# Two layers of graph message passing: which tensor the node update stores, where x2 and the residual base are formed, and how far ahead sources are prepared

## The reference, cut to what matters

```
h  = relu(layernorm(x));   x2 = x + rgcn(rgcn(h))     # each rgcn layer ends in a relu
h  = relu(layernorm(x2))
for each edge: msg = layernorm(relu(relu([h[src], h[dst], edge] @ eW1 + eb1) @ eW2 + eb2)) * eg + ebeta
agg = segment_sum(msg, dst)
upd = relu([h, agg] @ nW1 + nb1) @ nW2 + nb2
out = x2 + layernorm(h + upd) * ng + nbeta
```

## Time and profile before

| | us |
|---|---|
| median of 3 runs | 2960.8 (2960.65 to 2963.27) |
| profiled execution, its own time | 2965.21 |
| span of the profile | 2963.5 |
| node update, first load issued to the message pass's first gather | 1546.1 to 1841.2 |
| message pass, up to the last pass's first load | 1841.2 to 2549.3 |
| last node pass | 2549.3 to 2963.5 |

### The profile page before, as it was taken

One profiled execution on the slowest core, in us unless ns is written; L12 is line 12 of the kernel. 1 busy time (PEld: TensorE's weight loads), 2 busy tenths in 40 slices (PEclk: granted clock), 3 DMA queues, 4 the chain that ended last, 5 costly groups with the idle time before them and its releaser, 6 DMA issues. The chain is left out here.

```text
span 2963.5 us, 56389 instructions
## 1 busy us (share of the span) xinstructions
PE 2203.0 (74%) x16219; PEld 1880.8 (63%) x16219; DVE 2125.7 (72%) x7344; ACT 1585.1 (53%) x3382; POOL 2016.0 (68%) x1479
## 2 busy tenths in 40 slices
PE   4778988888578898888835665677777777566765
PEld 4678988888578898888835554444444444454553
DVE  6878877777333677666628775677777777499999
ACT  5996655555333444444417766444444443467774
POOL 6754777655667288888767773688877776455555
PEclk9999999999889999999978888899998988799998
DMA  7985555555389545555439998345444443466663
GB/s 245 313 287 132 108 103 101 99 86 95 39 319 365 177 86 86 87 87 86 77 66 400 412 409 324 84 85 94 84 91 84 84 91 50 144 192 191 197 197 131
DMA packets 268196, 473.22 MB, mean 160 GB/s; under 512 B 62736, under 2 KB 142288, under 8 KB 268112
## 3 DMA queue, kind: packets, MB, share of 16 engines
q1 hardware_dynamic: 158352, 382.24, 39.4%
q0 software_dynamic: 109760, 90.00, 20.0%
HBM read 291.28 MB, written 180.81 MB: 159 GB/s over the span
## 5 line engine op out<-in xcount | busy, mean ns | idle before, releaser
L1135 POOL DMA_INDIRECT s<-E_summed,c_scat x392 | 654.2, 1669 | 285.8 <-ACT E_summed L1314 164.9
L1363 PE MATMUL ps<-c_w,E_masked 128*128 128x128 f32 x6272 | 722.1, 276 | 3.2 <-DVE E_masked L1166 3.2
L1363 PEld LDWEIGHTS ps<-c_w,E_masked 128*128 128x128 f32 x6272 | 713.6, 193 | 4.0 <-DVE E_masked L1166 4.0
L1166 DVE SCALAR_TENSOR_TENSOR E_masked<-E_type_row,E_hT 128x512 f32<-128x512 int32 x784 | 484.6, 688 | 79.4 <-ACT E_hT L1283 66.9
L366 POOL DMA_INDIRECT E_src_rows<-s,c_src x392 | 414.9, 1058 | 166.5 <-issue 118.0
L1473 POOL DMA_INDIRECT s<-E_summed,c_scat x196 | 320.9, 1637 | 107.9 <-issue 56.4
L366 POOL DMA_INDIRECT E_src_rows<-in_x,c_src x196 | 192.9, 984 | 103.5 <-issue 74.2
L1462 POOL DMA_INDIRECT E_ends<-x,c_near x196 | 198.2, 1011 | 95.7 <-issue 57.3
L1314 ACT COPY E_summed<-ps 128x512 f32<-128x512 f32 x98 | 57.5, 586 | 374.9 <-DMA s<-E_summed,c_scat 374.9
L572 PE MATMUL ps<-c_sl,N_hT 128*128 128x128 f32 x1568 | 199.9, 282 | 18.1 <-DVE N_out L407 13.0
L1378 PE MATMUL ps<-E_msg,E_same 128*128 128x128 bf16 (+1 forms) x2450 | 207.3, 241 | 1.3 <-DVE E_msg L1216 1.3
(11 more groups left out here) (142 smaller groups left out, 4787.5 us busy)
## 6 DMA issues: line engine op xcount, KB each, us to landing
s<-N_out SPq DMA_DIRECT2D x147, 512.0 KB, 4.9
N_xin<-in_x SPq DMA_DIRECT2D x98, 512.0 KB, 13.1
N_sin<-s SPq DMA_DIRECT2D x98, 512.0 KB, 5.6
E_dst_row<-in_dst_line SPq DMA_DIRECT2D x147, 256.0 KB, 4.8
E_type_row<-in_type SPq DMA_DIRECT2D x98, 256.0 KB, 3.9
N_xin<-s SPq DMA_DIRECT2D x49, 512.0 KB, 6.1
x<-N_x SPq DMA_DIRECT2D x49, 512.0 KB, 11.3
N_xin<-x SPq DMA_DIRECT2D x49, 512.0 KB, 4.0
```

The source lines that it names most:

```text
L1135: pool.indirect_dma_start(s, bass.IndirectOffsetOnAxis(ap=c["scat"][:, k:k + 1], axis=0), summed[:, g % 2, t * D:(t + 1) * D], None, compu ...
L1166: nc.vector.scalar_tensor_tensor(out=masked[:, u % 2, r, :], in0=type_row[:, u, :], scalar=float(r), in1=hT[:, u % 2, :], op0=ALU.is_equal ...
L1363: ins = nc.tensor.matmul(ps[:, 2 + u % 2, t * D:(t + 1) * D], masked[:, u % 2, r, t * P:(t + 1) * P], w[:, r, :], start=(r == 0 and t == 0 ...
```

## The change

The node update forms x2 in place of s2, lets ScalarE normalise all eight rows with the relu in it, and stores h instead of x2. The copies of the product move from ScalarE to VectorE. Statistics are no longer kept. SP's order and the wait ahead of a load change.

The message pass gathers h for the destination ends, so only the four source tiles are normalised, and these now two groups ahead. SP also loads s2 and x again, group by group; VectorE forms x2 (`update`) and adds nbeta (`add_nbeta`), and SP stores the result as `base`. The turn of the next group comes ahead of the out layer on TensorE. The order on ScalarE and VectorE changes, and the buffer of sums is four deep. GpSimd's list of gathers and scatters is the same.

The last node pass loads h, s3 and base. GpSimd and the activations that formed h are gone. TensorE transposes into one pair of banks and has three pairs for the sums; ScalarE normalises all eight rows; VectorE multiplies by ng and adds the base, a group later. Base and result buffers are two deep. It is written out without a loop. Of the other stages only the zero fill of the tables' last rows changes: its source is 128 columns, read five times.

```diff
-                sp.dma_start(a[s][NODES:ROWS_S, :].rearrange("(p k) d -> p (k d)", k=DUMP_FOLD),
-                             zeros[:]).then_inc(loaded, 16)
+                sp.dma_start(a[s][NODES:ROWS_S, :].rearrange("(p k) d -> p k d", k=DUMP_FOLD),
+                             each_tile(zeros, DUMP_FOLD)).then_inc(loaded, 16)
             for out, in_ in loads:
...
             def load(i, u):
-                wait(sp, x2_ready, UNROLL * i + u - 3)
+                wait(sp, h_ready, UNROLL * i + u - 3)
                 sp.dma_start(sin[:, u, :], rows(a["s2"], node_base(i, u))).then_inc(loaded[u], 16)
                 sp.dma_start(xin[:, u, :], rows(a["x"], node_base(i, u))).then_inc(loaded[u], 16)
-            def store_x2(i, u):
+            def store_h(i, u):
                 g = UNROLL * i + u
                 if isinstance(g, int) and g == GROUPS_N - 1:
...
+                sp.dma_start(rows(a["h"], node_base(i, u)), h[:, u, :]).then_inc(h_stored[u], 16)
...
                         load(0, k)
-                m, n = ahead(i, u, -2), ahead(i, u, 4)
-                store_x2(i, u)
+                    store_h(0, 0)
+                m, l, n = ahead(i, u, -1), ahead(i, u, 1), ahead(i, u, 4)
                 if n:
                     load(*n)
+                if l:
+                    store_h(*l)
                 if m:
                     store(*m)
             sweep(sp, step)
-            for g in (GROUPS_N - 2, GROUPS_N - 1):
...
+            def scales(i, u):
+                ln.reciprocals(nc, dve, u, UNROLL * i + u)
+                ln.shifts(nc, u)
+            def results(i, u, half):
+                g = UNROLL * i + u
+                if half == 0:
+                    wait(dve, stored[u % 2], 16 * (2 * i + u // 2))
+                dve.wait_ge(product, 2 * g + half + 1)
+                nc.vector.tensor_copy(out[:, u % 2, half * 512:(half + 1) * 512],
+                                      ps[:, 4 + 2 * (u % 2) + half, :]).then_inc(out_ready, 1)
             def step(i, u):
                 if first(i, u):
-                    updated(0, 0)
-                    halves(0, 0)
...
+                        if k < 2:
+                            scales(0, k)
                 n, m = ahead(i, u, 3), ahead(i, u, 2)
                 if n:
-                    both(n, m)
-                elif m:
-                    reciprocals(*m)
-                    ln.shifts(nc, UNROLL * m[0] + m[1])
-                    normalise(*m, range(NT - ON_ACT)).then_inc(normed, 1)
+                    updated(*n)
+                if m:
+                    scales(*m)
+                if n:
+                    g = UNROLL * n[0] + n[1]
+                    halves(*n)
+                    ln.sums(nc, dve, g)
+                results(i, u, 0)
+                if n:
+                    ln.means(nc, dve, n[1], g)
+                results(i, u, 1)
+                if n:
+                    ln.totals(nc, dve, n[1], g)
             sweep(dve, step)
...
                 act.wait_ge(ln.shift_ready, g + 1)
-                wait(act, turned, 2 * (g - 1))
-                for k in range(NT - ON_ACT, NT):
+                wait(act, turned, 2 * (g - 3))
+                wait(act, h_stored[u], 16 * i)
+                for k in range(NT):
                     cols = slice(k * D, (k + 1) * D)
-                    ins = ln.scaled(nc, h[:, u % 2, cols], x2[:, u, cols], k, g, ACT.Identity)
-                ins.then_inc(act_normed, 1)
+                    ins = ln.scaled(nc, h[:, u, cols], sin[:, u, cols], k, u, ACT.Relu)
+                ins.then_inc(h_ready, 1)
...
+            def load(g):
+                u = g % UNROLL
+                wait(sp, product, 2 * (g - 3))
+                sp.dma_start(sin[:, u, :], rows(a["s3"], at(g))).then_inc(loaded[u], 16)
+                sp.dma_start(hin[:, u, :], rows(a["h"], at(g))).then_inc(loaded[u], 16)
+            def load_base(g):
+                u = g % 2
+                wait(sp, out_ready, 2 * (g - 1))
+                sp.dma_start(base[:, u, :], rows(a["base"], at(g))).then_inc(based[u], 16)
...
+            for g in range(GROUPS_N):
+                if g + 4 < GROUPS_N:
+                    load(g + 4)
+                if g >= 1:
+                    store(g - 1)
+                    if g + 1 < GROUPS_N:
+                        load_base(g + 1)
...
+            for g in range(GROUPS_N):
+                if g + 2 < GROUPS_N:
+                    hidden_rows(g + 2, 0)
+                ln.deviations(nc, act, c["eps"], g % UNROLL, g)
+                if g + 2 < GROUPS_N:
+                    hidden_rows(g + 2, 1)
+                outer_norm(g)
...
+            for g in range(GROUPS_N):
+                residual(g, 0)
+                if g + 1 < GROUPS_N:
+                    turn(g + 1)
+                residual(g, 1)
+                update(g, 0)
+                update(g, 1)
...
+            def scale(g, half):
                 cols = slice(half * 512, (half + 1) * 512)
-                nc.vector.tensor_tensor(res[:, u, cols], res[:, u, cols], base[:, u, cols],
+                dve.wait_ge(normed, 2 * g + half + 1)
+                if half == 0:
+                    wait(dve, out_ready, 2 * g)
+                nc.vector.tensor_tensor(tiles_of(scaled[:, cols]), tiles_of(normal[:, g % 2, cols]),
+                                        each_tile(c["ng"], NT // 2), ALU.mult).then_inc(scaled_ready, 1)
+            def finish(g, half):
+                u = g % 2
+                cols = slice(half * 512, (half + 1) * 512)
+                if half == 0:
+                    dve.wait_ge(based[u], 16 * (g // 2 + 1))
+                    wait(dve, stored[u], 16 * (g // 2))
+                dve.wait_ge(scaled_ready, 2 * g + half + 1)
+                nc.vector.tensor_tensor(res[:, u, cols], scaled[:, cols], base[:, u, cols],
                                         ALU.add).then_inc(out_ready, 1)
...
+            for g in range(GROUPS_N):
+                halves(g)
+                statistics(g)
+                if g:
+                    scale(g - 1, 0)
+                scales(g)
+                if g:
+                    scale(g - 1, 1)
+                    finish(g - 1, 0)
+                    finish(g - 1, 1)
...
+            def load_base(i, u):
+                wait(sp, base_stored[u % 2], 16 * (2 * i + u // 2))
+                sp.dma_start(base[:, u % 2, :], rows(a["s2"], node_base(i, u))).then_inc(base_loaded[u % 2], 16)
+                sp.dma_start(base_x[:, u % 2, :], rows(a["x"], node_base(i, u))).then_inc(base_loaded[u % 2], 16)
+            def store_base(i, u):
+                g = UNROLL * i + u
+                last_store(sp, base_stored, g)
+                sp.wait_ge(base_step, 2 * g + 2)
+                sp.dma_start(rows(a["base"], node_base(i, u)), base[:, u % 2, :]).then_inc(base_stored[u % 2], 16)
             def step(i, u):
                 if first(i, u):
                     for k in range(3):
                         load(0, k)
-                n = ahead(i, u, 3)
+                    load_base(0, 0)
+                m, n, l = ahead(i, u, 1), ahead(i, u, 3), ahead(i, u, -1)
                 if n:
                     load(*n)
+                if l:
+                    store_base(*l)
+                if m:
+                    load_base(*m)
             sweep(sp, step)
+            store_base(GROUPS_N // UNROLL, 0)
...
                     pool.indirect_dma_start(
-                        ends[:, u, GE + t * D:GE + (t + 1) * D], None, a["x2"],
+                        ends[:, u, GE + t * D:GE + (t + 1) * D], None, a["h"],
...
                         a["s3"], bass.IndirectOffsetOnAxis(ap=c["scat"][:, k:k + 1], axis=0),
-                        summed[:, g % 2, t * D:(t + 1) * D], None, compute_op=ALU.add).then_inc(added, 16)
+                        summed[:, g % UNROLL, t * D:(t + 1) * D], None, compute_op=ALU.add).then_inc(added, 16)
...
                 wait(dve, act_normed, UNROLL * i + u - 3)
-                lx.variances(nc, dve, [ends[:, u, t * D:(t + 1) * D] for t in range(2 * GT)], u, UNROLL * i + u)
-            def normalise(i, u):
+                lx.variances(nc, dve, [ends[:, u, t * D:(t + 1) * D] for t in range(GT)], u, UNROLL * i + u)
+            def scales(i, u):
                 lx.reciprocals(nc, dve, u, UNROLL * i + u)
                 lx.shifts(nc, u)
-                for t in range(GT, 2 * GT):
-                    tile = ends[:, u, t * D:(t + 1) * D]
-                    ins = lx.normalise(nc.vector, tile, tile, t, u)
-                ins.then_inc(normed, 1)
+            def update(i, u):
+                dve.wait_ge(base_loaded[u % 2], 32 * (2 * i + u // 2 + 1))
+                nc.vector.scalar_tensor_tensor(out=base[:, u % 2, :], in0=base[:, u % 2, :], scalar=0.0,
+                                               in1=base_x[:, u % 2, :], op0=ALU.max, op1=ALU.add).then_inc(base_step, 1)
+            def add_nbeta(i, u):
```

(31 more changed lines are left out.)

403 lines of the change are left out of this document (129 added, 274 removed).

## The result

The changed kernel takes 2857.0 us in the median of four runs (2854.4 to 2859.3), the one before 2960.7 beside it (2959.5 to 2963.3): ratio 0.9651, 95% interval 0.9639 to 0.9663. The prediction was 2850 us, range 2815 to 2905. The profiled execution of the changed kernel has a span of 2853.5 us against 2963.5, 110 us less. I cut both spans at the same marks, read from the time lines: GpSimd's first gather of the node update (0.7 us after the first load), the first gather of the message pass, the last pass's first load.

A forecast was written before the change was run, and what follows sets the result against it. Transfers were taken to bound the node update, GpSimd's issues (95% occupied) the message pass, with compute close, and VectorE, waiting for GpSimd, the last pass. Terms 0 + 2 + 2 - 115 = -111 us gave 2850 us, range 2815 to 2905.

The forecast's parts named there:

- Zero fill: At the very start: 512-byte pieces in place of 2.5 KB ones, costed at 0, bounds -1 to +1 us.
- Node update: Node update stage: transfers set the pace, so 0, plus 2 us for the tail; bounds -5 and +20 us.
- Message pass, compute side: Message pass: the compute engines need 13.0 to 13.8 us a group, taken as 13.3, against 13.6 now.
- The waits for sums: Message pass, GpSimd: its 21 us of waits for sums go, since compute at 13.3 us a group no longer limits it.
- the 2 us foreseen: Message pass: prologue 2 us earlier, with half the statistics ahead of the first turn.
- Message pass, GpSimd: Message pass: GpSimd's work goes from 661 to 665 us, +4, or +2 with the prologue; bounds -20 and +31.
- twice the work of that kind adds 0 to 18 us; I take 6: Message pass: more two-input VectorE operations lengthen GpSimd's scatter issues by 0 to 18 us, taken as 6.
- The waits for landing: Message pass: added transfers raise GpSimd's waits for scatters to land from 13.7 us to 30, between 14 and 47.
- Rival 3: Message pass loses 35 to 45 us by low clock and added VectorE work, or by scatter waits: 2890 us, chance 0.11.
- its own criterion: Prediction is wrong if the last pass takes over 320 us or the message pass moves by more than 30.
- Last pass: Last node pass: without GpSimd's work, 5.7 us a group (bounds 5.4 and 6.5), 299 us against 414, so -115.
- Rival 1: Last pass: transfers bind it at 6.4 us a group, so the stage takes 333 us and the total 2884; chance 0.16.

The follow-up runs named there:

- b_form: Kernel before, with the dump-row fill reading 128 columns of zeros five times and the tile kept at 640 columns, so no buffer moves: ratio 0.9972.
- a_none: Changed kernel without any base work in the message pass (no loads, VectorE operations or store); last pass loads h instead: 2780 us, stage 635.8 us.
- a_nodve: Changed kernel without VectorE's two operations on the base rows in the message pass, all transfers kept: 50 us faster by medians.
- a_gathers4: Changed kernel with all four gathers of a group issued ahead of all four scatters in the message pass: 2809 us, 48 us faster in the median.
- a_n3_noscale: Changed kernel without VectorE's product by ng in the last pass: tail 269.9 us, median 4.4 us below that of the changed kernel.
- b_nopool3: Kernel before, without GpSimd's two operations in the last pass: the tail falls from 421.5 to 298.3 us.
- a_pieces: Changed kernel with each of VectorE's two operations on the base rows cut into four pieces: runs of 2802.8, 2803.6, 2832.4 and 2838.1 us.

## Why the prediction was right, and where not

**Zero fill, 0 (bounds -1 to +1): wrong.** It is worth 8 us. The step looked only at what the fill delays at the start, and that is indeed nothing: the first edge pass begins its scatters at 258.7 us in the kernel before and in b_form.

**Node update, +2: -1.8, right.** The transfers are as full as before (DMA share 1.03 at 417 GB/s); the later loads cost nothing that shows.

**Message pass, compute side: right as far as it can be seen.** The waits for sums, 21 us, were to vanish: with the new order alone 6.2 are left (a_none). That a_none gains 24 is not this term alone, since 9 of it are waits for landing. What the compute side needs by itself was not measured, since GpSimd set the pace in every kernel. TensorE is idle ahead of the pair sums, as foreseen (103.6 us), but still ahead of the turn too, for gathers (64.1). The stage starts its scatters 38.7 us after its first gather instead of 41.1; the kernels made from the changed one need 38.7 to 43.4, so the 2 us foreseen can't be told.

**Message pass, GpSimd, +4: wrong, +60 from first to last scatter, and twice the upper bound.** The time lines divide the 60: issues +39 where I had 6, waits for landing +34 where I had 16, waits for sums -10 where I had -21. The step that failed is "twice the work of that kind adds 0 to 18 us; I take 6". Scaling an average by the amount of VectorE's work missed that an issue waits for the end of the operation under which it begins: the old two-input operations last 0.7 us, the new ones 1.2, and no issue was over by more than 0.6 before and by more than 1.1 after. The scatter went up by 79 ns and the gather by 124: 196 x 0.079 + 172 x 0.124 = 37 us, and the late source gathers 2 more. The gather's part I had not counted at all, since I read the excess from the scatter alone. The Trainium skill's rule (SBUF — State Buffer, "SBUF: two separate sides"), which I had set aside as "mostly not hit", is what the time line shows: each of the 60 issues begun under one of the two operations waits it out, the gather of 2.04 us among them, and a_nodve shows that without these the issues are as short as before.
The waits for landing, taken at 30 us with 47 as upper bound, were 48.2 over the whole stage: mechanism right, size just over the bound. Of the waits for sums, which were to go, 11 us stayed. Whether it was a second error to treat the two costs as independent terms isn't settled: the profiled runs say so, the medians don't. What is shown is that the transfers cost so much through the slack of 2.6 us that the scatters have: with 5.2 the landing waits are 9.9 us (a_gathers4).
Rival 3, a message pass that loses 35 to 45 us, came nearest in this stage; but of its causes the scatter waits (48.2 us in 49 groups, 1.0 a group) were only half. The low clock at the pair sums came in part: the granted clock of the stage fell from 0.90 to 0.85, and their products of 512 columns take 857 ns on the mean instead of 706. It did not set the pace, since GpSimd waits for sums only 11 us and TensorE itself waits for gathers. By its own criterion (the pass moves by more than 30) this part of the prediction was wrong.

**Last pass, -115: right in mechanism, -142 in size.** What was to vanish did: shift 0.17 us, adds 0.68. The period is 5.16 us, below the bound of 5.4. Of my 5.7 the sum of the instructions, 5.1, was right. The 0.3 for VectorE's waits on its own results is not there: 223.6 of 230 us are busy, small operations of neighbouring steps fill the gaps. The transfers do 2.10 MB in those 5.16 us, 406 GB/s, above the 390 I took, and VectorE hardly waits for them. The 0.3 for three limits of one height was also nothing; that loads four groups ahead absorb the jitter would explain it, but wasn't tried. 48 x 0.54 = 26 us of the 27; the start (12.8 us to the first statistic instead of 14), the last group (8.3) and the landing (3) were right. Rival 1, transfers that hold the pass at 6.4 us a group, is refuted by the 5.16 us, and a_n3_noscale goes to 5.00 with the same transfers.

**The sum.** -111 against -110 is luck: the stretches were off by -23, -4, +55 and -27 us, and these cancel.

## What to carry to other kernels

Price VectorE work that is added beside GpSimd's DMA issues by its longest instruction and by both kinds of issue, not by an average. Cutting it into pieces helps, but pieces without a gap can still be waited out together. When the order of a queue leaves a fixed slack between a transfer and its need, look at what is issued around it before adding bytes: moving two gathers ahead of two scatters was worth half of what the change itself brought. A moved piece of work can be right in its new stage only once that stage has been tuned for it: the 84 us that the base work cost in the profiled stage came down to 15.

## What the runs showed that I had not expected

- An indirect DMA's issue on GpSimd is held up to 1.1 us by a VectorE operation of 1.2 us with both inputs in SBUF: it waits for the end of the operation under which it begins. A VectorE operation on PSUM (0.40 us in both b_nopool3 and before) is not affected by GpSimd.
- A core moved 400 to 418 GB/s over stretches of 140 to 230 us.
- The shape of three small transfers at the start changed the time of an edge pass hundreds of microseconds later by 8 to 10 us.
- One and the same kernel can settle at two times 30 us apart (a_pieces: 2803 and 2835), at granted clocks of 0.93 and 0.92; why is open.
